# A graph block on one core: one fp32 down-projection in place of three products, normalised probabilities, column strips, and a new order of the units

## The reference, cut to what matters

```python
nx = _ln(x, ln1_g, ln1_b)                       # x: (128, 128, 256)
q, k, v = (nx @ w + b, split in 8 heads of 32)  # w = wq, wk, wv
bias = jnp.where(adj > 0, 0.1 * adj * adjf, -jnp.inf)[:, None]
scores = jnp.einsum('bhqd,bhkd->bhqk', q, k) / np.sqrt(32) + bias
out = jnp.einsum('bhqk,bhkd->bhqd', jax.nn.softmax(scores, axis=-1), v)
x1 = x + (out @ wo + bo)
n2 = _ln(x1, ln2_g, ln2_b)
return x1 + jax.nn.gelu(n2 @ w1 + b1, approximate=False) @ w2 + b2
```

## Time and profile before

| | |
|---|---|
| median of three runs (lowest, highest) | 1781.69 us (1774.5, 1782.0) |
| profiled execution: span | 1774.1 us (the run nearest to it took 1774.5) |
| TensorE matmuls busy | 1676.1 us, 94%, 11836 records |
| VectorE busy | 1295.6 us, 73% |
| ScalarE busy | 899.1 us, 51% |
| GpSimd busy | 475.9 us, 27% |
| granted TensorE clock, mean | 0.966 |
| ScalarE idle before L719, by the stack copies | 76.4 us |
| low parts of the hidden values (L940), VectorE | 174.4 us, 256 times 692 ns |
| high parts of the hidden values (L719), ScalarE | 156.0 us, 256 times 622 ns |
| GpSimd's `rstd`: add and power | 202 and 1022 ns |

### The profile page before, as it was taken

The page is one execution under the profiler, slowest core; times in us unless marked ns, Lnnn a source line. Parts: engine busy times, 40 slices in busy tenths (PEclk is TensorE's granted clock), DMA queues, the critical chain, the costliest instruction groups (busy, mean ns, idle before and its releaser), DMA issues.

```text
span 1774.1 us, 32603 instructions
## 1 busy us (share of the span) xinstructions
PE 1676.1 (94%) x11836; PEld 1544.7 (87%) x11836; DVE 1295.6 (73%) x2387; ACT 899.1 (51%) x1416; POOL 475.9 (27%) x392
## 2 busy tenths in 40 slices
PE   5789999999999999999999999999999999999998
PEld 4678988898988898988898988898998898898887
DVE  3677767787777787767787777788767788777773
ACT  2335555445555445555454555545555554555542
POOL 2332123333123333123333113333213333212300
PEclk8679999999999999999999999999999999999999
DMA  6323434423443423443422443432443432343300
GB/s 184 72 52 86 102 81 91 91 64 76 101 94 77 100 57 73 101 95 77 101 66 64 101 95 80 98 72 64 95 98 77 98 83 57 90 98 80 78 13 24
DMA packets 85803, 146.43 MB, mean 83 GB/s; under 512 B 9488, under 2 KB 60944, under 8 KB 85776
## 3 DMA queue, kind: packets, MB, share of 16 engines
q1 hardware_dynamic: 85776, 146.06, 35.7%
HBM read 28.58 MB, written 16.78 MB: 26 GB/s over the span
## 4 chain that ended last, share of the span: by engine, by line
DVE 40%; SPq 21%; PE 11%; issue 11%; DMA 8%; ACT 5%; POOL 2%; DVEq 1%; ACTq 0%; POOLq 0%
SPq L327 21%; DMA stack<-hid_parts 8%; DVE xhat L909 7%; DVE rmax L823 6%; DVE soft L820 6%; DVE hid_parts L928 4%; PE work L374 3%; PE work L375 3%; PE work L376 3%; DVE st L879 2%; DVE xhat L898 2%; ACT hid L708 2%; DVE xt_lo L920 2%; POOL rstd L1022 2%; ACT hid_parts L719 2%
## 5 line engine op out<-in xcount | busy, mean ns | idle before, releaser
L940 DVE TENSOR_TENSOR hid_parts<-hid,hid_parts 128x512 fp32r<-128x512 f32 x256 | 174.4, 692 | 281.8 <-ACT hid_parts L719 281.8
L1019 POOL TENSOR_TENSOR ve<-mv,eps 128x4 f32<-128x4 f32 x64 | 12.9, 202 | 1246.6 <-DVE mv L884 949.3
L374 PE MATMUL work<-w_hi,hid_parts 128*128 128x256 f32 x1024 | 294.6, 288 | 0.0
L375 PE MATMUL work<-w_lo,hid_parts 128*128 128x256 f32 x1024 | 283.6, 277 | 0.0
L376 PE MATMUL work<-w_hi,hid_parts 128*128 128x256 f32 x1024 | 283.6, 277 | 0.0
L458 PEld LDWEIGHTS mixed<-vals,probt 128*128 128x128 f32 x2048 | 242.8, 194 | 2.3 <-ACT probt L643 2.2
L458 PE MATMUL mixed<-vals,probt 128*128 128x33 f32 x2048 | 243.0, 274 | 1.4 <-ACT probt L643 1.4
L653 ACT ACTIVATE soft<-soft 128x1024 f32<-128x1024 f32 x128 | 135.4, 1058 | 169.8 <-DVE soft L825 168.2
L708 ACT ACTIVATE hid<-work,b_col 128x512 f32<-128x512 f32 x256 | 174.8, 684 | 72.1 <-PE work L376 72.0
L374 PE MATMUL work<-nt_hi,w_hi 128*128 128x512 f32 x512 | 203.6, 398 | 3.4 <-ACT hid L708 1.9
L376 PE MATMUL work<-nt_hi,w_lo 128*128 128x512 f32 x512 | 200.5, 392 | 0.0
(11 more groups left out here) (95 smaller groups left out, 3544.7 us busy)
## 6 DMA issues: line engine op xcount, KB each, us to landing
stack<-hid_parts SPq DMA_DIRECT2D x384, 256.0 KB, 5.0
xin<-in_x SPq DMA_DIRECT2D x32, 512.0 KB, 3.8
out<-res SPq DMA_DIRECT2D x128, 128.0 KB, 1.7
adj_in<-in_adj SPq DMA_DIRECT2D x32, 256.0 KB, 4.0
res<-in_L_gnn_w SPq DMA_DIRECT2D x1, 1024.0 KB, 8.2
soft<-in_L_gnn_w SPq DMA_DIRECT2D x1, 1024.0 KB, 10.6
x<-in_L_gnn_wq SPq DMA_DIRECT2D x1, 256.0 KB, 4.0
x<-in_L_gnn_wk SPq DMA_DIRECT2D x1, 256.0 KB, 4.4
```

The costliest lines, as they stand in the source:

```text
L374: pe.matmul(o, lhs_hi, rhs_hi, start=first, stop=False)
L375: pe.matmul(o, lhs_hi, rhs_lo, start=False, stop=False)
L940: dve.tensor_tensor(hid_lo[:, m, :], hid[:, m % 3, :], hid_hi[:, m, :].bitcast(F32), ALU.subtract).then_inc(hid_lo_ready, 1)
```

## The change

- The down-projection is one fp32 product per part of the hidden dimension, `hid` times `w2_all`, eight to a strip, in place of 24 fp32r ones. `hid` keeps all eight parts in fp32; `hidden_hi`, `hidden_lo` and the split of `w2` go. `qk_parts` has memory of its own.
- The probabilities are normalised before they are turned: the maximum is taken negated and goes into the exponential as its bias, the exponential is eight instructions, one a head, each also giving its sum, and VectorE multiplies by the reciprocals (`normalise`, now on 128x1024). `turn` waits for that (`normed`). `soft` has two buffers by the slot's parity. `turn_attn` goes: `mix` now has the values as weights and writes each head as 32 partitions by 128 columns, in one of four column strips.
- `work` has three banks; `mixed` and `wout` share one.
- The orders are new: `down(3)` and `result(3)` go to slot 3, the x transposes to slot 0, the n transposes to slot 1; `stats1` and `norm1` are done for group n+2 in slot 3; the values copy goes from ScalarE to VectorE; GpSimd starts a step with `residual_start` and `edges`. SyncE's list is not changed, but for the load of `w2`.

```diff
-UNITS = ([("down", 0, -2), ("down", 1, -2)]
-         + [("down", 2, -2), ("down", 3, -2)]
+UNITS = ([("down", 0, -2)]
+         + [("down", 1, -2), ("down", 2, -2)]
          + [("qk", 0, 1), ("qk", 1, 1), ("qk", 2, 1), ("qk", 3, 1)]
-         + [("v", 0, 1), ("v", 1, 1)] + [("up", m, -1) for m in range(FC)])
+         + [("v", 0, 1), ("v", 1, 1), ("down", 3, -2)] + [("up", m, -1) for m in range(FC)])
+BANKS = 3
...
+        hid = sb("hid", [P, FC, TOK])
+        qk_parts = sb("qk_parts", [P, 4, GB, DC, P], F32R)
...  PE: turn, mix, down
-                pe.wait_ge(prob_ready, step.graphs(s, 1))
+                pe.wait_ge(normed, step.graphs(s, 1))
...
-                for kind, slot, off in (("xt", 1, 1), ("nt", 2, -1)):
+                for kind, slot, off in (("xt", 0, 1), ("nt", 1, -1)):
                     if s == slot + 1 and step.has(off):
                         pe.wait_ge(taken[kind], step.count(off, DC, DC - 1))
...
+                    pe.wait_ge(x1_summed, step.graphs(s, 2))
                 for h in range(H):
-                    mm = pe.matmul(mixed[:, h * VW:(h + 1) * VW], probt[:, h, :],
-                                   vals[:, par, b, h, :], start=True, stop=True)
+                    j, c = h % RPB, h // RPB
+                    mm = pe.matmul(mixed[j * HD:(j + 1) * HD, c * P:(c + 1) * P], vals[:, par, b, h, :],
+                                   probt[:, h, :], start=True, stop=True, tile_position=(0, j * HD))
...
-                    mm = three(work[:, bank_of("down", b), 0:D], hid_hi[:, m, cols], hid_lo[:, m, cols],
-                               w2_hi[:, m, :], w2_lo[:, m, :], m == 0, m == FC - 1)
+                    mm = pe.matmul(work[:, bank_of("down", b), 0:D], hid[:, m, cols], w2_all[:, m, :],
+                                   start=(m == 0), stop=(m == FC - 1))
...  PE: body, new
+                score(0), turn(0), project_out(0), down(0), mix(0), flip "xt" 0, 1
+                score(1), turn(1), project_out(1), down(1), mix(1), down(2), flip "nt" 0, 1
+                score(2), turn(2), project_out(2), query_key(0), (1), mix(2), query_key(2), (3)
+                score(3), turn(3), project_out(3), values(0), (1), mix(3), down(3), up(0) to up(7)
...  ACT: exponential
+                for h in heads:
+                    a = act.activation(soft[:, par, h, :], soft[:, par, h, :], ACT.Exp,
+                                       bias=nmax[:, par, h:h + 1], accum_out=rsum[:, par, h:h + 1])
...  DVE: softmax, normalise
+                dve.tensor_reduce(nmax[:, par, :], soft[:, par, :, :], AX.X, ALU.max,
+                                  negate=True).then_inc(max_ready, 1)
...
+                dve.reciprocal(rinv[:, par, :], rsum[:, par, :]).then_inc(sum_inverted, 1)
+                dve.wait_ge(sum_inverted, step.graphs(s, 0))
+                dve.tensor_tensor(soft[:, par, :, :], soft[:, par, :, :],
+                                  rinv[:, par, :].rearrange("p (h a) -> p h a", a=1).to_broadcast([P, H, P]),
+                                  ALU.mult).then_inc(normed, 1)
...  DVE: body, new
+                softmax(0), residual(0), result(0), attn_lo(0), normalise(0), flip_lo "xt"
+                softmax(1), residual(1), result(1), attn_lo(1), norm2, normalise(1), result(2), flip_lo "nt"
+                softmax(2), residual(2), query_key_lo(0), (1), attn_lo(2), normalise(2), query_key_lo(2), (3)
+                softmax(3), residual(3), values_copy(0), (1), stats1, attn_lo(3), normalise(3), norm1, result(3)
...  POOL: result_start, body
-                pool.wait_ge(x1_summed, step.count(-1, GB, GB - 1))
+                pool.wait_ge(nhat_ready, step.count(-1, GB, GB - 1))
...
+                edges_wait(step)
+                residual_start(step)
+                edges(step)
                 rstd(step, -1, n_stats, mv2, ve2, n_veps, rstd2, n_rstd)
-                edges_wait(step)
                 result_start(step)
-                edges(step)
+                rstd(step, 2, x_stats, mv1, ve1, x_veps, rstd1, x_rstd)
```

More of the change, by code:

```diff
@@ L66, in bank_of @@
 def bank_of(kind, i):
[L67 removed]
+    return PLACE[(kind, i)] % BANKS
 class Step:
@@ L450, in mix @@
                 b = (s - 1) % GB
+                if not step.steady and step.n == 0 and s == 1:
+                    pe.wait_ge(bo_added, 1)
                 pe.wait_ge(turned_taken, step.graphs(s, 1) * 2)
@@ L672, in flip_hi @@
                        .then_inc(hi_taken[kind], 1)
-            def values_copy(step, half):
-                if not step.has(1):
-                    return
-                act.wait_ge(full["v"], step.count(1, 2, half))
-                if not step.steady and step.n == -1:
-                    act.wait_ge(ones_set, 1)
-                act.activation(
-                    vals[:, step.parity_of(1), half * 2:half * 2 + 2, :, 0:HD],
-                    work[:, bank_of("v", half), :].rearrange("p (b h d) -> p b h d", b=2, h=H),
-                    ACT.Copy).then_inc(taken["v"], 1)
             def query_key_copy(step, m):
@@ L808, in softmax @@
                     return
-                par = step.parity_of(0)
-                if not step.steady and step.n == 0 and s == 0:
-                    dve.wait_ge(lo_made, 7)
+                edges_par, par = step.parity_of(0), s % 2
                 dve.wait_ge(scores_full, step.graphs(s, 0))
@@ new lines, in normalise, with values_copy @@
+                dve.tensor_tensor(soft[:, par, :, :], soft[:, par, :, :],
+                                  rinv[:, par, :].rearrange("p (h a) -> p h a", a=1).to_broadcast([P, H, P]),
+                                  ALU.mult).then_inc(normed, 1)
+            def values_copy(step, half):
+                if not step.has(1):
+                    return
+                dve.wait_ge(full["v"], step.count(1, 2, half))
+                dve.tensor_copy(
+                    vals[:, step.parity_of(1), half * 2:half * 2 + 2, :, :],
+                    work[:, bank_of("v", half), :].rearrange("p (b h d) -> p b h d", b=2, h=H)
+                    ).then_inc(taken["v"], 1)
@@ L872, in stats1 @@
             def stats1(step):
-                if not step.has(1):
+                if not step.has(2):
                     return
-                par = step.parity_of(1)
-                dve.wait_ge(x_loaded[par], step.loads(1))
+                par = step.parity_of(2)
+                dve.wait_ge(x_loaded[par], step.loads(2))
                 for b in range(GB):
@@ L932, in query_key_lo @@
                 if not step.steady and step.n == -1:
[L933 to L941 removed]
+                    if m <= DC:
+                        late_lo(m)
             def result(step, b):
@@ L954, in body @@
             def body(step):
[L955 removed]
                 softmax(step, 0)
+                residual(step, 0)
                 result(step, 0)
[L959 removed]
+                attn_lo(step, 0)
                 normalise(step, 0)
[L961 removed]
+                flip_lo(step, "xt")
+                softmax(step, 1)
+                residual(step, 1)
                 result(step, 1)
[L963 to L973 removed]
                 attn_lo(step, 1)
                 norm2(step)
+                normalise(step, 1)
+                result(step, 2)
+                flip_lo(step, "nt")
                 softmax(step, 2)
+                residual(step, 2)
                 query_key_lo(step, 0)
                 query_key_lo(step, 1)
+                attn_lo(step, 2)
                 normalise(step, 2)
[L981 to L982 removed]
                 query_key_lo(step, 2)
                 query_key_lo(step, 3)
[L985 removed]
                 softmax(step, 3)
[L988 to L993 removed]
+                residual(step, 3)
+                values_copy(step, 0)
+                values_copy(step, 1)
+                stats1(step)
+                attn_lo(step, 3)
+                normalise(step, 3)
+                norm1(step)
+                result(step, 3)
+                if not step.steady and step.n == -1:
                     late_biases()
                     late_rows()
[L997 removed]
             dve.wait_ge(cols_loaded, 16)
@@ L1000, in _ @@
             dve.wait_ge(g1_ready, 1)
+            before = Step(-2, -1, 0, groups, False)
+            stats1(before)
+            norm1(before)
+            setup()
             steps(dve, groups, body)
```

245 lines of the change are left out of this document (78 added, 167 removed).

## The result

The changed kernel takes 2128.2 us (median of four runs, 2121.2 to 2130.5) against 1781.9 us in the runs beside it: a ratio of 1.1955, with a 95% interval of 1.1923 to 1.1987. It is slower by a fifth. 2210 us were forecast, with 2085 to 2305 as the range.

A forecast was written before the change was run, and what follows sets the result against it. TensorE's stream and SyncE's stack copies were taken to run neck and neck; store 3, made late, would delay the copies. 128.2 + 29 steps x 67.6 + 111.6 = 2200, plus 10 for start and tail: 2210 us, range 2085 to 2305.

The forecast's parts named there:

- The end of query_key 3: TensorE from a step's first score to the end of query_key 3: 36.0 us, where it took 34.5 before.
- The strips' lower end: A mix on TensorE with four strips at once: 0.43 us; one after another 1.70, and the middle, 1.07, was taken.
- The low clock behind the long wait: TensorE at the head of a step, after nearly 10 us idle for the copies: 2.9 us lost to low clock.
- Behind turn 1: Low clock on TensorE after the 2.1 us of idleness in slot 1: 1.4 us a step.
- The wait at turn 1: TensorE in slot 1 idles for VectorE's normalised probabilities and the x strips' lows: 2.1 us a step.
- VectorE from query_key 3 to the end of `norm1`: VectorE's softmax 3, residual, values copy, statistics and norm1 after query_key 3: from 36.0 to 49.4 us of the step.
- Copies to scores: From the first stack copy's issue on SyncE to the next step's first scores on TensorE: 17.4 us, unchanged.
- Rival 2: Strips do nothing, mix stays at 1.70 us: +0.63 x 3 a step, 2265 us; chance 0.23 together with rival 3.
- Rival 3: VectorE's normalise(1) waits out GpSimd's add into res: +1.8 us a step, 2262 us; chance 0.23 together with rival 2.
- Rival 4: Queue held less long: clock not lost, norm1 undisturbed, or strips at 0.43; each alone 2085 to 2155 us; chance 0.26.
- Rival 1: TensorE stays the bound, copies landing before the up-projections end: step 55 us, or 51.5 with strips at once; chance 0.06.
- the edits booked at nothing: Dropped hidden_hi/hidden_lo, eight exponentials (2 to 4.4 us, 2.9 taken), two soft buffers, earlier stats, missing w2 split: no step cost.

The follow-up runs named there:

- copies_first: Changed kernel with SyncE issuing the twelve stack copies ahead of store 3: 1847.4 us, ratio 1.0382 to the kernel before.
- down3_back: Changed kernel with down 3 and result 3 moved back to slot 1, behind down 2 and result 2: 1888.8 us, ratio 1.0597 to the kernel before.
- one_strip: Changed kernel whose steady steps write all eight heads of mix to column strip 0, result not the reference's: 2230.5 us, ratio 1.2528 to the kernel before.
- norm_alone: Changed kernel with GpSimd's add into x1 waiting until norm1 on VectorE is done: 2122.8 us, ratio 1.1929 to the kernel before.
- clock_kept: Changed kernel with 36 throw-away matmuls on TensorE before the wait for the copies in steady steps: 2129.7 us, ratio 1.1975 to the kernel before.
- new_order: copies_first with result 3 ahead of norm1, TensorE work put before its waits in slots 1 and 2, and VectorE reordered: 1690.9 us, 0.9512 of the kernel before.
- strip_in_a_row: Changed kernel with mix's heads ordered 0 4 1 5 2 6 3 7, one strip's four records in a row: 2135.2 us, ratio 1.2008 to the kernel before.

## Why the prediction was right, and where it was off

The mechanism was right. The copies are issued 0.5 us behind store 3, which waits for a `result(3)` behind `norm1`; the scores follow 17.4 us later; TensorE idles 9.6 us there (10 forecast). copies_first and down3_back take this cause away in two ways, and 281 and 239 us come back. One reading was too kind: TensorE already waited 0.5 us for the copies in the kernel before, so any delay of them is paid in full, and not only one of more than half a microsecond.

The total was 82 us too high, 4%. The measured time lies in the range, but outside the 2165 to 2245 of the forecast as it stood, to which 0.45 was given. By its own terms, in a step of 67.6 forecast and 64.85 measured:

- The end of query_key 3: 36.0 forecast, 1146.68 - 1114.52 = 32.2 measured. Three mixes at 0.58 in place of 1.07 are 1.5 of the 3.8. The strips' lower end, 0.43, was nearer than the middle; the estimate from the Trainium skill's 2.38 for three strips (section Part 3 of "TensorE: Matmul & The Clock Gate"), 0.71, was nearer too, and four strips gave 3.2 times (one_strip).
- The low clock behind the long wait: 2.9 forecast, 1.8 + 0.3 measured. Behind turn 1: 1.4 forecast, nothing measured. Together 2.2. This term was taken from two stretches before and carried over as a fixed price; norm_alone and clock_kept show that it is not one. It moves between the places where TensorE waits.
- The wait at turn 1: 2.1 forecast, 1.66 measured; turn 2: 0.6 and 0.82. A down strip: 3.55 and 3.55.
- VectorE from query_key 3 to the end of `norm1`: 13.4 forecast, 14.3 measured, since `norm1` took 4.12 in place of 3.74 and the rest was 0.5 longer. From there to the first copy 0.8 and 1.0. Copies to scores 17.4 and 17.4. These 1.1 us too few hid part of the 3.8 too many.

Rival 2 (strips do nothing) is refuted by one_strip. Rival 3 expected `normalise(1)` to wait out GpSimd's add. It took 1.22 us as alone, and GpSimd's add was the one that became longer, 3.44 against 2.38: they started 0.01 us apart. The lock of which the Trainium skill speaks ("SBUF — State Buffer", section "Who interferes with whom") goes to whoever starts first, which is in line with this row; the rival had the wrong loser. Rival 4, 2085 to 2155 with 0.26, is where the truth lay by size. It was no single one of its cases: the strips near their lower end, and half of the low clock, while `norm1` was disturbed in full. Rival 1 is true of no kernel here as long as SyncE's order stands; with the order changed, new_order's step of 49.9 is below its 51.5.

Of the edits booked at nothing, the exponentials came out near the 2.9 us taken, for which the prediction showed no row. Each of the 1024 has a second instruction that reads the sum, as the upper end of 4.4 supposed, but it overlaps the next exponential:

```profile
L626 ACT ACTIVATE soft<-soft,nmax 128x128 f32<-128x128 f32 x1024 | 396.4, 389 | 116.4 <-DVE nmax L767 116.0
L626 ACT ACTIVATION_READ_ACCUMULATOR soft<-soft,nmax 128x1 f32 x1024 | 191.8, 187 | 0.0
```

From start to start of two heads are 0.39 us, 3.1 for eight, and in the step shown VectorE never waits for their sums.

## What to carry to other kernels

When work is moved on one engine, read the list of every queue that waits for its result, and of everything behind that wait: here an untouched DMA queue, in which a store had become late, held twelve copies that had nothing to do with it. That cost 281 us, three times what the best order of these runs gains on the kernel before. A cover is used up from both sides: what shortens the work beside a transfer needs the transfer to start earlier. And an edit that shows no difference has not been shown to be off the path: look in the trace whether it took effect, and where its gain was given back.

## What the runs showed of the hardware

- The granted clock can absorb a gain. The changed kernel, norm_alone, clock_kept and most steps of strip_in_a_row all take 64.7 to 64.9 us a step, though `norm1` is 2.7 us shorter in one and the head 2 us faster in another; the low stretches grew or moved by nearly as much. When a wait of 1.7 to 2.0 us is followed by a low clock and when not is left open, and so is why the steps of all four agree this closely.
- Column strips work for fp32 products of 32 columns: sixteen records in 0.58 us against 1.87 in one strip, whatever the order of the heads.
- An fp32 product of 128x128 by 128x256 takes 0.44 us at full clock, 3.54 for eight, against 0.35 for three fp32r products (2.83 for 24).
